# Third cross-attention of a fused transformer on one core: all scores of a batch at once on four row tiles, maxima, exponentials and flips by quarters, and ScalarE's last copy behind the next batch's first exponentials

## The reference, cut to what matters

```python
def _attn(q, k, v):
    qh = q.reshape(B, Lq, HEADS, HEAD_DIM)
    kh = k.reshape(B, Lk, HEADS, HEAD_DIM)
    vh = v.reshape(B, Lk, HEADS, HEAD_DIM)
    scores = jnp.einsum('bqhd,bkhd->bhqk', qh, kh) * SCALE
    probs = jax.nn.softmax(scores, axis=-1)
    out = jnp.einsum('bhqk,bkhd->bqhd', probs, vh)
    return out.reshape(B, Lq, HIDDEN)
...
x = x + _L2_xattn_ref(_layernorm(x, axis=-1), ctx_1024, ctx_1024)
```

## Time and profile before

| what | value |
|---|---|
| median of 3 runs | 2756.11 us (2754.11 to 2757.16) |
| time of the profiled execution | 2755.86 us |
| its span in the profile | 2754.1 us |
| mean granted TensorE clock over the span | 0.966 |
| TensorE matmul busy | 2501.2 us, 91% of the span |
| VectorE busy | 1668.2 us, 61% |
| ScalarE busy | 1379.4 us, 50% |
| GpSimd busy | 720.6 us, 26% |

### The profile page before, as it was taken

The page is one execution under the profiler, slowest core; times in us unless marked ns, Lnnn a source line. Parts: engine busy times, 40 slices in busy tenths (PEclk is TensorE's granted clock), DMA queues, the critical chain, the costliest instruction groups (busy, mean ns, idle before and its releaser), DMA issues. The chain is left out here.

```text
span 2754.1 us, 84228 instructions
## 1 busy us (share of the span) xinstructions
PE 2501.2 (91%) x36457; PEld 2129.0 (77%) x36457; DVE 1668.2 (61%) x3213; ACT 1379.4 (50%) x3278; POOL 720.6 (26%) x1042
## 2 busy tenths in 40 slices
PE   7999998999968999999999867996998878999988
PEld 6888666777756899999997657995777757999577
DVE  6877675666656333333324674657776866777663
ACT  3888424554532544444442234434886445787342
POOL 3232202211102300000000303432345726666300
PEclk9999999999989999999999978997999999999999
DMA  3110002212021100000000042325320003111000
GB/s 99 36 34 25 1 16 84 64 33 64 3 77 47 48 17 17 17 17 17 2 2 25 3 135 89 127 81 187 95 83 1 3 3 102 51 54 45 1 1 31
DMA packets 118225, 126.74 MB, mean 46 GB/s; under 512 B 10877, under 2 KB 110152, under 8 KB 117864
## 3 DMA queue, kind: packets, MB, share of 16 engines
q1 hardware_dynamic: 114024, 110.93, 13.1%
q0 software_dynamic: 3840, 10.49, 1.2%
HBM read 105.67 MB, written 15.73 MB: 44 GB/s over the span
## 5 line engine op out<-in xcount | busy, mean ns | idle before, releaser
L1157 ACT ACTIVATE s_ca_probs<-s_ca_scores,s_ca_neg_max 128x256 f32<-128x256 f32 x512 | 235.5, 480 | 20.9 <-DVE s_ca_neg_max L1203 14.7
L2484 DVE COPY s_mx_w_mixed<-s_mx_ps 128x512 f32<-128x512 f32 x256 | 163.7, 684 | 94.5 <-PE s_mx_ps L2330 81.1
L2439 ACT COPY s_mx_w_mixed<-s_mx_ps 128x512 f32<-128x512 f32 x256 | 137.4, 589 | 107.7 <-PE s_mx_ps L2317 85.9
L1203 DVE TENSOR_REDUCE s_ca_neg_max<-s_ca_scores 128x4 f32<-128x1024 f32 x128 | 155.7, 1218 | 33.1 <-PE s_ca_scores L1060 19.9
L82 PE MATMUL s_cc_shared<-s_cc_ctxT_low,h_cc_wkv_high 128*128 128x256 f32 x512 | 145.9, 285 | 2.2 <-DVE s_cc_ctxT_low L1807 2.2
L300 POOL TENSOR_SCALAR x_normed_transposed<-x_normed_transposed,h_cc_rstd,h_cc_shift 128x256 f32<-128x256 f32 x56 | 30.8, 559 | 446.3 <-PE s_cc_out L1701 271.4
L83 PE MATMUL s_cc_shared<-s_cc_ctxT_high,h_cc_wkv_low 128*128 128x256 f32 x512 | 144.6, 282 | 0.0
L84 PE MATMUL s_cc_shared<-s_cc_ctxT_high,h_cc_wkv_high 128*128 128x256 f32 x512 | 144.4, 282 | 0.0
L1073 PE MATMUL s_ca_probs_flipped<-identity,s_ca_probs 128*128 128x128 f32 x1024 | 140.6, 280 | 0.9 <-ACT s_ca_probs L1157 0.9
L1765 ACT COPY s_cc_kT<-s_cc_shared 128x512 f32<-128x512 f32 x128 | 75.1, 586 | 117.8 <-PE s_cc_shared L84 117.8
L1073 PEld LDWEIGHTS s_ca_probs_flipped<-identity,s_ca_probs 128*128 128x128 f32 x1024 | 109.5, 141 | 25.7 <-issue 17.8
(11 more groups left out here) (590 smaller groups left out, 7946.1 us busy)
## 6 DMA issues: line engine op xcount, KB each, us to landing
h_ca_ctxT<-in_ctxT SPq DMA_DIRECT2D x96, 256.0 KB, 3.2
h_mx_w_by_input<-in_L_ffn_eW1T SPq DMA_DIRECT2D x16, 512.0 KB, 5.5
h_mx_w_by_hidden<-in_L_ffn_eW2T SPq DMA_DIRECT2D x8, 1024.0 KB
h_re_win<-in_L_ffn_W_in SPq DMA_DIRECT2D x8, 1024.0 KB, 6.0
h_ca_ctx<-in_ctx SPq DMA_DIRECT2D x32, 256.0 KB, 2.8
x_normed_transposed<-in_ctx SPq DMA_DIRECT2D x7, 1024.0 KB, 5.3
h_re_wout<-in_L_ffn_W_out SPq DMA_DIRECT2D x8, 512.0 KB, 3.8
choice_results<-s_rt_zeros SPq DMA_DIRECT2D x4, 1024.0 KB, 10.6
```

Of the source, the lines that this page charges most:

```text
L1157: last = nc.scalar.activation(PR[b % 2][:, p, :], psS[:, p // 2, (p % 2) * NKEY:(p % 2 + 1) * NKEY], ACT.Exp, bias=nmax[b % 2][:, p:p + 1] ...
L1203: nc.vector.tensor_reduce(nmax[b % 2][:, 4 * n:4 * n + 4], psS[:, 2 * n:2 * n + 2, :].rearrange("p r (g k) -> p r g k", g=GR), AX_X, ALU.m ...
L2439: last = nc.scalar.copy(part(int(name[1]), r), bank(j, r))
L2484: last = nc.vector.tensor_copy(part(int(name[1]), r), bank(j, r))
```

## The change

All scores of a batch are now issued together over the four row tiles, once all exponentials of the batch before are done (`s_e >= 4 * b`); a semaphore goes up for each bank. Maxima are taken bank by bank, exponentials are signalled by quarters (two at a time), and flips are quarters too. TensorE does flips 0, 1, 2 of batch b, then the scores of b+1, then flip 3, the flip of a normed tile or the turn of the attended rows, and attend. VectorE copies quarters 0 and 1, ScalarE quarters 2 and 3. ScalarE copies quarter 3 behind the first two exponentials of batch b+1; the copy of the attended rows of b-1 moves to the head of the loop of b. VectorE's statistics move to the odd batches. GpSimd's addition goes behind its copy of the values. `FLIPS` has the quarters in a row, with the normed tile and the turned rows behind them. The amount of arithmetic is the same.

```diff
--- before.py
+++ after.py
@@ -1289,10 +1289,9 @@
 
     FLIPS = []
     for b in range(NB):
-        FLIPS += [("P", b, 0), ("P", b, 1)]
+        FLIPS += [("P", b, q) for q in range(4)]
         if b in TURN:
             FLIPS.append(("N", TURN[b], 0))
-        FLIPS += [("P", b, 2), ("P", b, 3)]
         if b and b % 2 == 0:
             FLIPS.append(("U", b // 2 - 1, 0))
     FLIPS.append(("U", TILES - 1, 0))
...
@@ -1360,11 +1359,11 @@
                 for b in range(NB):
                     if b + 2 < NB:
                         spread(b + 2)
-                    if b and b % 2 == 0:
-                        add(b // 2 - 1)
                     if b + 2 < NB:
                         pool.wait_ge(s_o, b + 1)
                         held.values(pool, b + 2)
+                    if b and b % 2 == 0:
+                        add(b // 2 - 1)
                     if b < KC:
                         ahead(pool, b)
                     if b >= 9 and b % 8 == 1:
@@ -1383,30 +1382,30 @@
                         elif kind == "U":
                             pe.wait_ge(s_od, n + 1)
                         else:
-                            pe.wait_ge(s_td if k % 2 else s_ta, 2 * n + k // 2 + 1)
+                            pe.wait_ge(s_ta if k // 2 else s_td, 2 * n + k % 2 + 1)
                     return bank(f)
 
-                def scores(b, n):
+                def scores(b):
                     pe.wait_ge(s_q, b + 1)
                     pe.wait_ge(s_ct[b % NCT], 16 * (b // NCT + 1))
                     if b:
-                        pe.wait_ge(s_e, 2 * (b - 1) + n + 1)
+                        pe.wait_ge(s_e, 4 * b)
                     for g in range(GR):
-                        for r in (2 * n, 2 * n + 1):
+                        for r in range(NR):
                             rows = slice(32 * r, 32 * r + 32)
                             last = nc.tensor.matmul(psS[:, r, g * NKEY:(g + 1) * NKEY], QB[b % 2][rows, g, :, :].rearrange("p h q -> p (h q)"),
                                                     CT[b % NCT][rows, g, :], start=True, stop=True)
-                    last.then_inc(s_s, 1)
-
-                def flip(b, n):
-                    pe.wait_ge(s_e, 2 * b + n + 1)
-                    for h in range(2):
-                        dst = claim(("P", b, 2 * n + h))
-                        for a in range(2):
-                            for c in range(2):
-                                k = 2 * a + c
-                                last = nc.tensor.transpose(dst[:, k * P:(k + 1) * P], PR[b % 2][:, 4 * n + 2 * h + a, c * P:(c + 1) * P], ident[:, :])
-                        last.then_inc(s_t, 1)
+                            if g == GR - 1:
+                                last.then_inc(s_s, 1)
+
+                def flip(b, q):
+                    pe.wait_ge(s_e, 4 * b + q + 1)
+                    dst = claim(("P", b, q))
+                    for a in range(2):
+                        for c in range(2):
+                            k = 2 * a + c
+                            last = nc.tensor.transpose(dst[:, k * P:(k + 1) * P], PR[b % 2][:, 2 * q + a, c * P:(c + 1) * P], ident[:, :])
+                    last.then_inc(s_t, 1)
 
                 def attend(b):
                     pe.wait_ge(s_vr, b + 1)
@@ -1433,36 +1432,33 @@
 
                 pe.wait_ge(s_w, 32)
                 pe.wait_ge(s_set, 2)
-                for n in range(2):
-                    scores(0, n)
+                scores(0)
                 keep_busy(nc, psO[:, 0:P], ident[:, :], 12)
                 for b in range(NB):
-                    flip(b, 0)
+                    for q in range(3):
+                        flip(b, q)
+                    if b + 1 < NB:
+                        scores(b + 1)
+                    flip(b, 3)
                     if b in TURN:
                         norm.flip(pe, TURN[b], claim(("N", TURN[b], 0))[:, :])
-                    if b + 1 < NB:
-                        scores(b + 1, 0)
-                    flip(b, 1)
                     if b and b % 2 == 0:
                         turn_attended(b // 2 - 1)
-                    if b + 1 < NB:
-                        scores(b + 1, 1)
                     attend(b)
                 turn_attended(TILES - 1)
 
             @block.scalar
             def _(act):
-                def exponentiate(b, n):
-                    act.wait_ge(s_mx, 2 * b + n + 1)
-                    for a in range(4):
-                        p = 4 * n + a
-                        last = nc.scalar.activation(PR[b % 2][:, p, :], psS[:, p // 2, (p % 2) * NKEY:(p % 2 + 1) * NKEY], ACT.Exp,
-                                                    bias=nmax[b % 2][:, p:p + 1])
+                def exponentiate(b, q):
+                    act.wait_ge(s_mx, 4 * b + q + 1)
+                    for g in range(GR):
+                        k = 2 * q + g
+                        last = nc.scalar.activation(PR[b % 2][:, k, :], psS[:, q, g * NKEY:(g + 1) * NKEY], ACT.Exp, bias=nmax[b % 2][:, k:k + 1])
                     last.then_inc(s_e, 1)
 
-                def turned(b, n):
-                    act.wait_ge(s_t, 4 * b + 2 * n + 1)
-                    nc.scalar.copy(PT[b % 2][:, 4 * n:4 * n + 2, :, :].rearrange("p a c q -> p (a c q)"), bank(("P", b, 2 * n))[:, :]).then_inc(s_ta, 1)
+                def turned(b, q):
+                    act.wait_ge(s_t, 4 * b + q + 1)
+                    nc.scalar.copy(PT[b % 2][:, 2 * q:2 * q + 2, :, :].rearrange("p a c q -> p (a c q)"), bank(("P", b, q))[:, :]).then_inc(s_ta, 1)
 
                 def attended(b):
                     i = b // 2
@@ -1471,30 +1467,34 @@
                         act.wait_ge(s_uf, i - 1)
                     nc.scalar.copy(UB[i % 2][:, :, (b % 2) * SEQ:(b % 2 + 1) * SEQ], psO[:, 0:4 * SEQ].rearrange("p (k q) -> p k q", k=4)).then_inc(s_u, 1)
 
-                for n in range(2):
-                    exponentiate(0, n)
+                for q in range(4):
+                    exponentiate(0, q)
                 for b in range(NB):
-                    turned(b, 0)
+                    if b:
+                        attended(b - 1)
+                    turned(b, 2)
+                    if b + 1 < NB:
+                        exponentiate(b + 1, 0)
+                    turned(b, 3)
                     if b in TURN:
                         norm.store(act, TURN[b], bank(("N", TURN[b], 0))[:, :])
-                    turned(b, 1)
                     if b + 1 < NB:
-                        exponentiate(b + 1, 0)
-                    attended(b)
-                    if b + 1 < NB:
-                        exponentiate(b + 1, 1)
+                        for q in range(1, 4):
+                            exponentiate(b + 1, q)
+                attended(NB - 1)
 
             @block.vector
             def _(dve):
-                def largest(b, n):
-                    dve.wait_ge(s_s, 2 * b + n + 1)
-                    nc.vector.tensor_reduce(nmax[b % 2][:, 4 * n:4 * n + 4], psS[:, 2 * n:2 * n + 2, :].rearrange("p r (g k) -> p r g k", g=GR),
-                                            AX_X, ALU.max, negate=True).then_inc(s_mx, 1)
-
-                def turned(b, n):
-                    dve.wait_ge(s_t, 4 * b + 2 * n + 2)
-                    nc.vector.tensor_copy(PT[b % 2][:, 4 * n + 2:4 * n + 4, :, :].rearrange("p a c q -> p (a c q)"),
-                                          bank(("P", b, 2 * n + 1))[:, :]).then_inc(s_td, 1)
+                def largest(b):
+                    for r in range(NR):
+                        dve.wait_ge(s_s, 4 * b + r + 1)
+                        nc.vector.tensor_reduce(nmax[b % 2][:, 2 * r:2 * r + 2], psS[:, r, :].rearrange("p (g k) -> p g k", g=GR),
+                                                AX_X, ALU.max, negate=True).then_inc(s_mx, 1)
+
+                def turned(b, q):
+                    dve.wait_ge(s_t, 4 * b + q + 1)
+                    nc.vector.tensor_copy(PT[b % 2][:, 2 * q:2 * q + 2, :, :].rearrange("p a c q -> p (a c q)"),
+                                          bank(("P", b, q))[:, :]).then_inc(s_td, 1)
 
                 def divide(i):
                     got = bank(("U", i, 0))[:, :].rearrange("p (h m k d) -> p h m k d", h=2, m=8, k=2)
@@ -1514,19 +1514,16 @@
 
                 dve.wait_ge(s_w, 32)
                 nc.vector.tensor_reduce(PAR[:, :], S16[:, :].rearrange("p (a h) -> p h a", h=2), AX_X, ALU.add).then_inc(s_par, 1)
-                for n in range(2):
-                    largest(0, n)
+                largest(0)
                 for b in range(NB):
-                    turned(b, 0)
+                    for q in range(2):
+                        turned(b, q)
                     if b + 1 < NB:
-                        largest(b + 1, 0)
-                    turned(b, 1)
+                        largest(b + 1)
                     if b and b % 2 == 0:
                         divide(b // 2 - 1)
-                    if b + 1 < NB:
```

(9 more changed lines are left out.)

## The result

The changed kernel takes 2766.44 us (median of 14 runs, 2760.33 to 2770.75) against 2756.81 (14 runs, 2754.11 to 2760.86): ratio 1.0031, 95% interval 1.0025 to 1.0038, so by the ratio 8.5 us slower (6.9 to 10.5); the two medians are 9.6 apart. The forecast was 2770.5, within 2760 to 2782.

A forecast was written before the change was run, and what follows sets the result against it. TensorE's work bounds the stage now; afterwards a serial ring through three engines, 6.10 us a batch against 5.59. 0.94 + 15.3 - 1.6 = 14.6 us slower, so 2770.5 us, range 2760 to 2782.

The forecast's parts named there:

- the ring through it: Serial chain per batch: scores, maximum, two exponentials, ScalarE's copy of quarter 3, attend, 12 flips; 6.10 us against 5.59.
- the ring through the exponentials: Second chain, from scores through all eight exponentials to the next scores: 5.47 us, to fit beside 6.10.
- the eight links: Steps from one batch's scores to the next: 1.18, 0.69, 0.03, 0.72, 0.61, 0.37, 1.04, 1.46 us.
- the link from the copy to attend: TensorE's wait after ScalarE's copy of quarter 3, two more semaphores behind it: 0.37 us, ends 0.15 and 0.37.
- No extra for a normed tile: In six batches ScalarE has 0.46 us more before six exponentials: 5.93, still under 6.10, priced at nothing.
- The ends: First and last batch of the stage: attend(0) 0.94 us late, last batch 4.0 to 4.1 for 5.69, 1.6 back.
- A: Rival: the serial chain is as drawn but short, 5.77 us or less, up to 4 us slower; chance 0.07.
- B: Rival: attend finds its copy ready, VectorE's load of 4.68 us a batch decides, 28 us faster; chance 0.06.
- C: Rival: holes in TensorE drop the granted clock to 1.2 GHz, 115 us slower, 2870; chance 0.04.
- D: Rival: four row tiles don't overlap with 256 columns, 7.16 us a batch, 46 us slower, 2802; chance 0.03.
- A sign read wrong: Sign of being right: TensorE idle some 1.5 us before each attend, put down to ScalarE's copy.
- the last 20 flips: Cited with the matmuls of rows 3 as showing TensorE has 1.1 us a batch to give once scores overlap.

The follow-up runs named there:

- Copy first: ScalarE copies quarter 3 ahead of the first exponentials of the next batch, against the changed kernel; stage 178.8 us, whole 0.9987 of the kernel before.
- copy later: ScalarE copies quarter 3 behind four exponentials instead of two, against the changed kernel; stage 219.8 us, whole 1.0145 of the kernel before.
- The exchange: Attend waits for VectorE's copies ahead of ScalarE's, two lines exchanged against the changed kernel; stage 193.1 us, whole 1.0036 of the kernel before.
- the second comparison: The changed kernel measured once more against the kernel before, nothing else changed; ratio 1.0025 (1.0015 to 1.0035), stage 188.9 us.
- the fastest version: Quarter 3 copied ahead of the exponentials and the normed tile copied by VectorE, against the changed kernel; 2749.47 us, 0.9973 of the kernel before.

## Why the prediction was right

- **The bound moved as said.** The scores at once cost 1.07 us of TensorE up to flip 3 (1983.61 to 1984.68), as forecast from the earlier trace rows, and the gain went into a hole before attend. Copy first, change and copy later differ in the place of one copy, and the gaps are 5.43, 5.79 and 6.53: in the last two the ring through it sets the pace, in the first the ring through the exponentials.
- **Seven of the eight links** were right within 0.04 us: 1.16 for 1.18, 0.68 for the maximum of one bank for 0.69, 0.05 to the exponentials for 0.03, 0.72, the copy 0.58 for 0.61, 1.03, 1.46.
- **The step that failed** is the link from the copy to attend: 0.37 forecast, 0.11 measured. I read the order of the waits off the source and took one more wait to be one more 0.11. The exchange shows that what counts is which instruction carries the wait: 0.11 and 0.25, with the same waits. At batch 0, whose row gave the 0.15, there was one instruction less: a single one carries the waits for both engines' copies. Over 30 rings this is 7.8 of the 14.6 forecast. The ring was 5.79, not 6.10, and the stage's cost came out 8.8 us too high (14.6 for 5.8).
- **No extra for a normed tile** failed with it: 5.93 was forecast for that ring and 6.00 measured, but it was to hide under 6.10. Five gaps at 0.21 are 1.05 us.
- **The ends**: start 10.16 from scores to attend against 9.69, 0.47 late for 0.94 (again the long link); last batch 3.92 for 4.0 to 4.1.
- **The sum by its own terms**: 0.47 + (174.82 - 167.70) - 1.77 = 5.8 us, toward the low end of the forecast's 4 to 26. The whole shows 8.5 (6.9 to 10.5) and, in the second comparison, 6.9 (4.1 to 9.7): 1 to 3 us more, of which only the first comparison is sure. They were in no step, and by luck they bring the forecast nearer than its sum was.
- **Rivals.** A (5.77) was nearly the ring that came, and for one of its reasons: the wait was short (0.11 for its 0.15). The maximum wasn't (0.68, not 0.61). B fell: VectorE's and ScalarE's loads never became the bound, not even in the fastest version (133.78 and 130.02 of 165 us). The Trainium skill, TensorEngine Tiling (Array Packing), PSUM Bottleneck, says only that the copy out of PSUM may become the bottleneck once TensorE is four times as fast; here the scores became twice as fast. In this ring the emptying of PSUM is on the path, but by its latency, while no engine that does it is full. C didn't happen at the holes of the change (1.1 to 1.6 us), nor at 1.3 to 1.7 with the waits exchanged, but does at 1.87 and 2.30 in the copy-later kernel. D fell: 16 passes over four row tiles take 1.15 us.
- **A sign read wrong**: the wait was to be put down to ScalarE's copy; the profile put it to "issue". Only the exchanged kernel names the copy. "Issue" stands in just those kernels in which, from batch 1 on, the second of the three instructions is the one that waits. And "the last 20 flips" that the prediction names beside rows 3 stand in no row; the 1.06 us come of rows 3 and 7.

## What to carry to other kernels

Before work is taken off a full engine, draw the ring that remains: with one set of buffers, each step of it is latency, and work that was free beside the full engine (two exponentials ahead of a copy) is now paid in every turn. Issue first what releases the next engine. Of several waits let the one that comes last stand in the last instruction, and read in the trace which that is: here the wait written third stood in the first. A change of 0.2% needs the stage's own time from two profiles, since the rest of a kernel can vary by more.

## What was not expected of the hardware

- With holes of 1.87 and 2.30 us in a 6.5 us period the granted clock fell to 0.5 for 3.4 us at six of 31 places, five times behind 2.30 and once behind 1.87; with holes of 1.1 to 1.6 us in 5.8 it never did. Fillers of about 1.3 us a batch made that kernel 9.9 us faster (2786.99 against 2796.9).
- The four waits before one matmul stood in three instructions, in another order than in the source. From the last signal to the matmul it was 0.11 us or 0.25, by which of the first two it met.
- One VectorE instruction of 512 columns took 0.43 us in the median and 3.7 beside a 4.1 us GpSimd instruction, in some executions of the same kernel; in the others the scan behind it took 3.38 in place of 1.22, beside the same instruction. The recurrent stage is 4 to 6 us longer in the first case (25.0 to 26.6 against 20.7 to 21.0, and 22.3 once). That the two engines share something is inferred from the times of their ends, 0.20 or 0.28 us apart in all twelve profiles; no run here takes GpSimd's instruction away.
